# GpSimd's 64 sends of routed rows, in portions of five that each wait for a pair's scores

## What is computed

```python
xn = _layernorm(x, axis=-1)
# attention, by chunks of 64 tokens, 16 heads of 8:
scores = jnp.where(causal, jnp.einsum('bthd,bshd->bhts', q_c, k_c), 0.0)
intra = jnp.einsum('bhts,bshd->bthd', scores, v_c)
S = S + jnp.einsum('bthd,bthe->bhde', v_c, k_c)
# experts: the token's expert is argmax(xn @ centroids.T)
h = jax.nn.relu(jnp.einsum('etd,efd->etf', xn_e, w1) + b1[:, None, :])
y = x[None, :, :] + jnp.einsum('etf,edf->etd', h, w2) + b2[:, None, :]
gated = a * y + (1.0 - a) * x[None, :, :]
x = x + attention(xn) + experts(xn)
```

## Time and profile before

| what | us |
|---|---|
| median of 3 timed runs | 474.2 (472.26 to 475.53) |
| the profiled execution's own time | 471.31 |
| its span, from the first to the last instruction | 469.5 |
| TensorE busy | 360.6 |
| VectorE busy | 287.6 |
| ScalarE busy | 244.0 |
| GpSimd busy | 251.2 |

### The profile page before, as it was taken

The page is one execution under the profiler, slowest core; times in us unless marked ns, Lnnn a source line. Parts: engine busy times, 40 slices in busy tenths (PEclk is TensorE's granted clock), DMA queues, the critical chain, the costliest instruction groups (busy, mean ns, idle before and its releaser), DMA issues. The chain is left out here.

```text
span 469.5 us, 17240 instructions
## 1 busy us (share of the span) xinstructions
PE 360.6 (77%) x6891; PEld 303.5 (65%) x6891; DVE 287.6 (61%) x771; ACT 244.0 (52%) x647; POOL 251.2 (53%) x244
## 2 busy tenths in 40 slices
PE   7879898879988441111069999975999999999992
PEld 6557666657756220000037777765999999999992
DVE  7967978866498300000027777773788877887871
ACT  4766777557647300000116666622776667776671
POOL 4573667626231777777600000000788888888885
PEclk9999999999989755555559999997999999999998
DMA  5124354640402111111112223313555555555430
GB/s 165 42 94 139 97 158 161 189 135 25 162 4 88 54 52 57 53 52 52 52 43 74 90 73 94 94 47 92 88 70 69 76 69 68 70 71 73 54 35 0
DMA packets 55150, 37.35 MB, mean 80 GB/s; under 512 B 5352, under 2 KB 51616, under 8 KB 55072
## 3 DMA queue, kind: packets, MB, share of 16 engines
q1 hardware_dynamic: 42800, 27.72, 20.1%
q0 software_dynamic: 12272, 8.54, 13.2%
HBM read 18.72 MB, written 17.97 MB: 78 GB/s over the span
## 5 line engine op out<-in xcount | busy, mean ns | idle before, releaser
L431 POOL DMA_INDIRECT out_dram<-qx,rows x71 | 112.6, 1586 | 119.4 <-DVE qx L913 97.5
L621 ACT ACTIVATE qx<-sc,b1T 128x128 f32<-128x128 f32 x284 | 81.3, 368 | 43.2 <-PE sc L1284 37.4
L386 POOL DMA_INDIRECT slots_d<-rows,pos_i x64 | 63.0, 984 | 29.9 <-issue 19.2
L1284 PE MATMUL sc<-wide,tokens 128*128 128x128 f32 x568 | 76.1, 277 | 0.2 <-ACT wide L615 0.2
L1292 PE MATMUL bank<-tokens,qx 128*128 128x128 f32 x568 | 75.1, 275 | 0.4 <-ACT qx L621 0.4
L761 DVE TENSOR_TENSOR pr<-sc,causal 128x1536 f32<-128x1536 f32 (+1 forms) x32 | 63.7, 1989 | 16.7 <-PE sc L1136 16.4
L1284 PEld LDWEIGHTS sc<-wide,tokens 128*128 128x128 f32 x568 | 69.9, 194 | 0.5 <-ACT wide L615 0.5
L1292 PEld LDWEIGHTS bank<-tokens,qx 128*128 128x128 f32 x568 | 69.0, 192 | 0.6 <-ACT qx L621 0.6
L752 DVE TENSOR_TENSOR vp<-bank,krs 128x512 f32<-128x512 f32 x16 | 11.1, 692 | 78.7 <-remote 74.7
L899 DVE COPY tokens<-xT 128x1024 f32 x71 | 56.4, 795 | 1.7 <-issue 1.6
L1190 PE MATMUL bank<-pr,vz 128*32 128x64 f32 x2048 | 40.8, 224 | 12.8 <-issue 10.1
(11 more groups left out here) (154 smaller groups left out, 563.2 us busy)
## 6 DMA issues: line engine op xcount, KB each, us to landing
rows<-slots_d SPq DMA_DIRECT2D x71, 66.0 KB, 2.0
slots_d<-empty SPq DMA_DIRECT2D x8, 528.0 KB, 4.1
res<-in_L_attn_x_dram SPq DMA_DIRECT2D x16, 256.0 KB, 3.0
out_dram<-res SPq DMA_DIRECT2D x16, 256.0 KB, 3.3
tokens<-in_L_attn_x_dram SPq DMA_DIRECT2D x7, 512.0 KB, 4.2
w1raw<-in_L_ffn_w_dram SPq DMA_DIRECT2D x8, 256.0 KB, 3.7
w2raw<-in_L_ffn_w_dram SPq DMA_DIRECT2D x8, 256.0 KB, 4.8
out_dram<-qx,rows POOLq DMA_INDIRECT x71
```

Source lines behind the costliest of these rows:

```text
L386: pool.indirect_dma_start(slots_d, bass.IndirectOffsetOnAxis(ap=pos_i[:, t:t + 1], axis=0), rows[:, t, :], None, bounds_check=NS * P - 1, ...
L431: pool.indirect_dma_start(out_rows, bass.IndirectOffsetOnAxis(ap=xs[:, a, D + 2:D + 3].bitcast(U32), axis=0), ye[:, a, :], None, bounds_ch ...
L621: last = nc.scalar.activation(ht[:, k % 2, c * P:(c + 1) * P], SC[2 + k % 2][:, c * P:(c + 1) * P], ACT.Relu, bias=b1T[:, bass.ds(e * FC + ...
L1284: last = mm(SC[2 + k % 2][:, c * P:(c + 1) * P], ws[:, k % 3, c * P:(c + 1) * P], xsT[:, k % 2, :], start=True, stop=True)
```

## The change

GpSimd's 64 sends, one loop before, become 14 groups, one for each pair from 18 to 31. Before group h GpSimd waits until TensorE has finished the scores of pair h (`sc_ps` at least h + 1), and then sends five tiles: `sent(h)` is how many have gone before it. Pairs 18 to 29 have five tiles each, pair 30 the last four, pair 31 none. The sends themselves, their order, their semaphores and every other engine's program are the same.

```diff
+        def sent(h):
+            return min(NT, 5 * (h - ROUTED))
...
-            for t in range(NT):
-                scatter_rows(t)
+            for h in range(ROUTED, NH):
+
+                pool.wait_ge(s("sc_ps"), h + 1)
+                for t in range(sent(h), sent(h + 1)):
+                    scatter_rows(t)
```

## The result

The changed kernel takes 460.7 us (median of 4 runs, 456.6 to 464.9), the kernel before 473.2 us beside it (4 runs, 469.6 to 475.5). The ratio is 0.972, with a 95% interval from 0.966 to 0.977; it leaves out the run of 464.9, which counts as one in a slower state. It is faster, but by 12.5 us where 67 were forecast. These are times of chips of one kind. On a chip of the other kind both kernels take 390 us, as the experiments found, and there is nothing to gain.

The account below looks back on a forecast made before the run. TensorE's crawl behind a queue of GpSimd's sends was taken as the bound: 86.2 us saved, 12 x 1.6 = 19.2 lost again, so 471.3 - 67.0 = 404.3, stated as 406 us for the median, range 385 to 466.

Parts of the forecast that it names:

- The bound: Attention half-steps of pairs 19 to 31: TensorE crawls while GpSimd sends routed rows, which costs 86.2 us.
- The hole: 14th to 20th slice of the profile: TensorE nearly idle at half clock, two half-steps taking 98.4 us; cost 86.2 us.
- Is it sending, or a queue of sends?: Routed-row sends against expert-stage sends: duty nearly the same, so the queue of waiting sends is the likeliest cause of the crawl.
- The toll: TensorE's loss for each portion of five sends: 1.6 us taken, 4.0 as upper bound; 12 x 1.6 = +19.2 us.
- the sum: 12 half-steps from pair 19 to 31: -86.2 and +19.2, together -67.0 us, giving 404.3 for the profiled execution.
- The hole gone: Between the scores of pairs 19 and 31: the stretch of near-idle TensorE disappears, -86.2 us.
- The waits at no cost: GpSimd's 14 waits for scores delay nobody; SyncE's first load of sorted rows is issued at 251.5, sends hidden.
- The granted clock: TensorE's half-steps: a granted clock of one half in each step would add to the loss per portion; no size given.
- Slower: Rival, 16%: each portion is a full crawl with a tail; slower from a tail of 0.43 us, 490 us with 2 us.
- No toll: Rival, 23%: the crawl needs a deep queue, which a portion never reaches; about 390 us by the median.
- a rule that speaks against the change: GpSimd's descriptor making: sending in one go is free, portions bring nothing; 471 to 474 us, chance as the 8% rival's.

Follow-up runs that it names:

- nosend: The kernel before without its 64 sends of routed rows, so the expert stage's rows stay empty: 383.3 us, against 474.2 for the kernel before on the same chip.
- before_b: The kernel before, unedited, run again with a trace on a chip where TensorE isn't held during the sends: 389.8 us (9 runs), the profiled one 392.9.
- addsend: The kernel before with its 64 sends given the add operation of the expert stage, which changes the output: 420.2 us.
- fill8_d: The kernel before with a GpSimd memset of 8 columns after each send, on a chip where TensorE is held: 474.5 us, beside 469.5 of the kernel before.
- filler: The kernel before with a GpSimd memset of 528 columns after each send, a send starting every 1.69 us: 416.7 us, beside 473.3 of the kernel before.
- after_b: The changed kernel, unedited, run again on a chip where TensorE isn't held during the sends: 389.1 us (8 runs), ratio 0.997 to the kernel before.

## Why the prediction was right and wrong

**The bound: right for the chips that it was read from.** The hole was the sends' doing (nosend, 91 us), and "the sends as its cause, though no row names a mechanism" stands. But the hole was taken for a property of the program. before_b has the same program and the same GpSimd rows without it.

**"Is it sending, or a queue of sends?": the step that failed.** I compared the two stages of sends by GpSimd's duty, 76% and 84%, found them alike, and took the queue for what differs. Three other things differ. The expert stage's sends add. The time from one send's start to the next is 1.28 us here and 120/64 = 1.9 us in the expert stage, and the expert stage's matmuls are busy end to end at 0.28 us each, so that a pause of 0.3 us in the handing over need not show. addsend has the deep queue and loses little, before_b has it and loses nothing. The changed kernel has at most six waiting and loses nearly all, and fill8_d has at most two and the whole hole. It is the spacing, filler against fill8_d.

**The toll: the term that was mis-sized.** 1.6 us per portion was taken, 4.0 held for the upper bound. Measured are (152.9 - 12 x 6.10)/12 = 6.6 us. The bound was no bound: the five sends it came from were the first of all, when TensorE still had instructions in hand (31 products at full pace), and I argued it down further by the queue. The whole 6.4 us that five sends take, with a tail, was the upper bound to use. All 64 sends fall into these 12 half-steps, 5.3 to each. In every second half-step TensorE also waits 1.6 to 1.8 us for VectorE's scaled values, 10.3 us in all; nosend and after_b don't have this wait, and the sum had no term for it.

**The hole gone: right.** -86.2 came in full, there is no stretch without work any more. But the toll of 12 x 6.64 = 79.7 us took nearly all of it: 6.5 us remain between pairs 19 and 31. The prediction said that tolls "up to 6 us would end near 460", and 460.7 came out. That is partly luck. By the sum a toll of 6.64 gives 464.8 for the profiled execution, which took 460.8, because it reached pair 19 4.6 us earlier, ahead of any send.

**The waits at no cost: right.** GpSimd's 77.9 us of waiting for scores delay nobody, and the slot loads follow the store at 306.84. The expert stage is unchanged, 1078 matmuls in 120 us. The first load came at 307.32 rather than 251.5: 60.5 us more of toll, less the 4.6 us by which pair 19 came earlier.

**The granted clock: right, as a part of the toll.** It was named as one: 0.76 in the stretch. Behind a portion scores can take more than twice as long (53 of them 2.48 us at 162.32, where 64 take 1.21 at 176.73).

**The rivals.** *Slower* had the mechanism nearly word for word, "TensorE does nothing while GpSimd sends, whatever waits", and its break-even at a tail of 0.43 us. The tail is about 1 us in the rows, yet the half-steps come to 152.9/12 = 12.7 and not over 13.3, because TensorE doesn't quite do nothing: it gets 26 products through in the portion shown, and it still has work in hand when the portion begins. So this rival's mechanism was the right one, at 16%; with a tail of 1 us its sum is 13.85 a half-step, 1.1 too high. *No toll* is what the one chip without the hold that ran the changed kernel shows, 389 us against this rival's 390, and there the kernel before has no hole either. Likewise for *a rule that speaks against the change*, on making descriptors (the Trainium skill, "DMA: Bandwidth & Descriptors", Anatomy of one DMA): by it sending in one go is free. On the one chip without the hold where both kernels ran the trace agrees, 0.997. With the hold it does not: 0.972 for the portions, and 91 us for the sends as a whole. GpSimd's own rows, the same in both, can't tell which.

## What to carry to other kernels

Indexed sends of GpSimd that follow each other every 1.3 us can bring TensorE to a standstill on some chips. Here they did so with two sends waiting and with 12, and with 16 bytes a row as with 528. Portions of them hardly help, since within a portion the spacing is the same. Other GpSimd work put between the sends, so that 1.7 us or more lie between two starts, gives most of the time back (417 against 473 us), and costs 20 us on a chip that doesn't have the hold. So time such a change on several chips before it is kept: neither this kernel nor any tried here is the best on all of them.

And when two stages are compared to find what makes one of them bad, write down everything that differs, the period from start to start too, before one difference is named the cause; an upper bound is to be taken from the worst that the rows allow, here the whole length of the sends and a tail.

## What the runs showed of the hardware that was not expected

- One program, one input: 470 to 474 us on three chips and 386 to 391 on three others, and within 1% of the median where it was repeated on one chip. The difference lies in the stretch of the indexed sends, at 12 half-steps in 159.4 or in 77.1 us.
- In the hold TensorE gets its instructions at intervals close to multiples of 0.70 us (fill8_d: starts at 171.44, 172.85, 174.97, 177.77), with a granted clock of 0.50.
- An indexed send costs GpSimd 0.97 us whether it moves 528 bytes a row, 16 bytes, or drops nearly all rows, with the add operation 1.54, and a plain one 0.54.
- The traces with the hold lack most of the sends' semaphore raises: 161 of 1024 on record in before, 988 in before_b.
- An instruction of 0.13 us between two indexed sends is free: the period stays 1.28 us, and it takes up part of the gap of 0.30.
